# Sandwich attention layer: a slot's scores and first projected piece ahead of its output tiles, on TensorE and VectorE

## The chip, the cores and the metric

The kernel runs on one core of a Trainium2 chip. Times are microseconds of device time for one execution; the median of several runs counts. Engine names: PE is TensorE's matmuls and PEld its weight loads, DVE is VectorE, ACT is ScalarE, POOL is GpSimdE, SP is SyncE, which issues nearly all DMAs.

## What is computed

One transformer layer in sandwich form on x of 4 x 512 x 512: attention with 32 query heads and 8 key/value heads of 128 (weights are 4-bit codes times a scale per group of 128 rows), then a gated feed-forward part of width 1376 with 8-bit weights. Each part has a layer norm in front and behind and is added to its input.

```
q, k, v = [xn @ ((codes - 8) * repeat(scales, 128))  for q, k, v]     # xn = layernorm(x)
q, k = rope(q), rope(k);  k, v repeated 4 times over the heads
attn = softmax(q @ k.T * 128**-0.5 + causal_mask)
x = x + layernorm((attn @ v) @ dequant(o))
xn = layernorm(x)
x = x + layernorm((silu(xn @ gate.T * gs) * (xn @ up.T * us)) @ down.T * ds)
```

## The kernel before

Every factor is held as a high and a low float16 half, so a product is two or three matmuls. The attention part is 32 units of work, a unit U being one key/value head for one batch b = U % 4. A unit has four slots h = 0 to 3, one for each query head n = 4U + h, 128 slots in all. The order of each engine's work in a slot is written out by hand, engine by engine, and the engines meet at semaphores.

In slot n TensorE does, in this order: attend for head n-2 (L891, probabilities times V, 30 matmuls of 128 columns into ps_o), the scores of head n+1 in three groups (L876, into three banks ps_s), four output tiles of an earlier head through the output weights (L870, two matmuls of 512 columns each, named O0 to O3), and one or two pieces of the next unit's projection (L838, eleven matmuls of 512 columns for K and Q0 to Q3; L854, 48 of 128 columns for V). The pieces are dealt out by `FULL` (L76): slot 0 has K and Q0, slot 1 has Q1, slot 2 has Q2 and V, slot 3 has Q3. In the last unit `LAST` (L77) puts turned rows Y and X in their place. The scores' groups and the first three tiles alternate, then come the pieces, then O3.

Tiles and pieces share `ps_p`, a ring of four PSUM banks. `slot_sequence` (L82) gives the order of the entries in a slot; `bank_of` (L100) gives entry e of a unit the bank (22 x parity + e) % 4, and `bank_free` (L945) lets TensorE wait until the entry four places back has been read: for a tile VectorE's addition into y (o_add), for a piece VectorE's second reading or, for V, its low half (piece_dve). O0 also waits for ot_in: the head's output must have been normalized (ScalarE L703, L707), split (GpSimdE L554, o_low) and transposed by a DMA that SyncE issues (L428).

VectorE in a slot: `lows` (L1210, reads the score banks), the additions `add_output` (L1203, L1208) of the tiles, a reciprocal (L1227), and `take` (L1176) for each rope piece: it reads the bank once into `other` (L1191) and once into `rot` (L1195). The second reading also waits for GpSimdE to be done with the `rot` buffer (`rope_low`, L532, L538, writes k_lo or q_lo from it). There are three such buffers: K and Q2 share one, Q1 and Q3 another. A piece's two halves are swapped by DMA, added on GpSimdE one slot later (L530), made into the high half on ScalarE (L668), and into the low half on GpSimdE two slots later, behind that slot's p_lo (L546) and o_low. In slot 1 GpSimdE also dequantizes a weight block (L561, L564). At the end of slot 3 VectorE makes the low half of a weight block (`w_low`, L1104, L1108); in batch 3 the next K projection waits for it.

Of the kernel before, what the change touches and what calls it, by code (L numbers as in the profile page):

```python
# [80 lines left out]

def slot_sequence(pieces):  # L82

    return ("O0", "O1", "O2") + pieces + ("O3",)


def sequence(slots):
# [7 lines left out]
def place(slots, h, name):  # L95

    return sum(len(slot_sequence(p)) for p in slots[:h]) + slot_sequence(slots[h]).index(name)
# [71 lines left out]
def layer(nc, x, w_codes, w_scales, o_codes, o_scales,  # L169
# [3 lines left out]
    with ctx:  # L173
# [649 lines left out]
        def _(pe):  # L823
# [116 lines left out]
            def unit(U, b, slots, last=False, first=False):  # L940
                r = b % 2
                names = sequence(slots)
                idle = place(slots, 3, "O0") if first else 0

                def bank_free(e):  # L945


                    if first and e < RING + idle:
                        skipped = [x for x, name in enumerate(names[:idle]) if name[0] == "O"]
                        used = [x for x in range(e) if x not in skipped and bank_of(r, x) == bank_of(r, e)]  # L950
                        pe.wait_ge(piece_dve, len(START) + sum(q[0] in "KVQ" for q in names[:used[-1] + 1]) if used
                                   else len(START))
                        return
                    back = e - RING
                    ahead = names[back] if back >= 0 else sequence(FULL)[back]
                    if back < 0:
                        tail = sequence(FULL)[back + 1:] if back < -1 else ()
                        outs = outs_before(U) - sum(q[0] == "O" for q in tail)
                        pieces = pieces_before(U) - sum(q[0] in "KVQ" for q in tail)
                    else:  # L960
                        outs = outs_before(U) + sum(q[0] == "O" for q in names[:back + 1])
                        pieces = pieces_before(U) + sum(q[0] in "KVQ" for q in names[:back + 1])
                    if ahead[0] == "O":
                        after(pe, o_add, outs)
                    elif ahead[0] == "Y":
                        pe.wait_ge(y_read, int(ahead[1]) + 1)
                    elif ahead[0] == "X":
                        pe.wait_ge(m_xlo, int(ahead[1]) + 1)
                    else:
                        pe.wait_ge(piece_dve, pieces)  # L970

                def out_tile(n, h, nt):
                    if first and h < 3:
                        return
                    e = place(slots, h, f"O{nt}")
                    bank_free(e)
                    if nt == 0:
                        pe.wait_ge(ot_in, 16 * (n - 2))
                    if h < 3:
                        output(U - 1, h + 1, (h + 1) % 2, nt, bank_of(r, e))  # L980
                    else:
                        if first:
                            pe.wait_ge(o_cent, 1)
                        elif b == 0 and nt == 0:
                            pe.wait_ge(o_cent, U + HG)
                        output(U, 0, 0, nt, bank_of(r, e))

                for h in range(HG):
                    n = U * HG + h
                    more = not (last and h == HG - 1)  # L990
                    nxt = (n + 1, U, r, h + 1) if h < HG - 1 else (n + 1, U + 1, (r + 1) % 2, 0)
                    if h > 1:
                        attend(n - 2, r, h % 2, pieces_before(U - 1) + START.index("V") + 1)
                    elif not first:
                        attend(n - 2, 1 - r, h % 2, pieces_before(U - 2) + START.index("V") + 1)
                    if more:
                        scores(*nxt, 0)
                    out_tile(n, h, 0)
                    if more:
                        scores(*nxt, 1)  # L1000
                    out_tile(n, h, 1)
                    if more:
                        scores(*nxt, 2)
                    out_tile(n, h, 2)
                    for piece in slots[h]:
                        e = place(slots, h, piece)
                        if first and h == 0:
                            pe.wait_ge(xt_lo, NT)
                        bank_free(e)
                        bank = ps_p[:, bank_of(r, e), :]  # L1010
                        if piece[0] == "Y":
                            turn_y(int(piece[1]), bank)
                        elif piece[0] == "X":
                            turn_xn(int(piece[1]), bank)
                        else:
                            if b == NB - 1 and piece == START[0]:
                                pe.wait_ge(w_lod, U + 5)
                            if piece == "V":
                                project_v(U + 1, (b + 1) % NB, bank_of(r, e))
                            else:  # L1020
                                project(U + 1, (b + 1) % NB, piece, bank_of(r, e))
                    out_tile(n, h, 3)

            unit(0, 0, FULL, first=True)
            unit(1, 1, FULL)
# [77 lines left out]
        def _(dve):  # L1103
# [216 lines left out]
            def unit(U, b, slots, last=False, first=False):  # L1320
# [10 lines left out]
                for h in range(HG):  # L1331
                    n = U * HG + h
                    hp = (h + 1) % 2
                    more = not (last and h == HG - 1)
                    for g in range(NG):
                        if more:
                            lows(n + 1, hp, g)
                        out_tile(h, g)
                    invert(n, h)
                    if last and h:  # L1340
                        rows_add(h - 1)
                    for piece in slots[h]:
                        if piece[0] == "X":
                            xn_low(int(piece[1]), ps_p[:, bank_of(r, place(slots, h, piece)), :])
                    for V, vpar, piece, bank, taken in made(U, r, h, slots):
                        if piece != "V":
                            take(V, vpar, piece, bank, taken)
                    out_tile(h, 3)
                    for V, vpar, piece, bank, taken in made(U, r, h, slots):
                        if piece == "V":  # L1350
                            take(V, vpar, piece, bank, taken)
                    if h == 3 and not last:
                        w_low(U + 5, exact=(b + 5) % KT == EXACT)
                    if last and h:
                        to_xn(h - 1)
                    if last:
                        rows_first(h)
# [132 lines left out]
```

## Time and profile before

| | us |
|---|---|
| median of 3 runs | 1477.96 (1477.52 to 1479.47) |
| the profiled execution | 1479.83, its span 1478.0 |
| TensorE busy | 1386.7 (94%) |
| VectorE busy | 1115.5 (75%) |
| GpSimdE busy | 996.5 (67%) |
| ScalarE busy | 987.1 (67%) |

TensorE is at nine tenths or more of nearly every slice between the start-up and the end. A busy share tells which engine to look at; what a change of order is worth is read from the waits of that engine and from the rows of single slots. In the rows of a timeline the columns are start in us, duration in us, engine, line, operation, out<-in with the shape, count, and in brackets the idle time of that engine before it and what ended it.

### The profile page before, as it was taken

The page shows a single profiled execution, that of the slowest core. Times are in us where ns is not written, and L with a number is a line of the kernel's source. Part 1 is how long each engine was busy: PE and PEld are TensorE (multiplying, and loading weights), DVE is VectorE, ACT ScalarE, POOL GpSimd, SP SyncE. Part 2 cuts the span into 40 slices and gives each one's busy share as a digit, 9 for nine tenths or more (in the row PEclk, how much of TensorE's full clock was granted, in tenths as well). Part 3 has the DMA queues.
Part 4 walks back from the last instruction along what each step waited for, and adds up shares of the span by engine and source line. Part 5 has one row for each costly group of instructions (what it writes and reads, how often), then busy time and mean ns, then how long its engine had stood idle before and what let it go on. Part 6 is the DMA issues. An engine that isn't in the chain of part 4 may idle for free.

```text
span 1478.0 us, 33061 instructions
## 1 busy us (share of the span) xinstructions
PE 1386.7 (94%) x10944; PEld 837.3 (57%) x10944; DVE 1115.5 (75%) x2480; ACT 987.1 (67%) x2582; POOL 996.5 (67%) x710
## 2 busy tenths in 40 slices
PE   3689999999999999999999999999999968999998
PEld 1455665656656666666666665666666643454543
DVE  7856787777777878777777877788878795686744
ACT  2468777777777878877877887778777853241321
POOL 2369888888878888888888888888888751010100
PEclk9899999999999999999999999999999988999999
DMA  7389999999998998998899989899999854011000
GB/s 231 80 171 173 172 173 179 171 189 178 186 171 180 170 177 171 171 174 165 166 167 180 173 171 172 172 169 187 175 165 179 154 104 81 16 43 51 8 30 29
DMA packets 523323, 217.09 MB, mean 147 GB/s; under 512 B 479280, under 2 KB 481424, under 8 KB 523152
## 3 DMA queue, kind: packets, MB, share of 16 engines
q1 hardware_dynamic: 520592, 210.74, 72.9%
q0 software_dynamic: 2560, 4.23, 1.7%
q8 instruction: 88, 1.44, 0.4%
q14 instruction: 83, 0.68, 0.2%
HBM read 55.44 MB, written 4.29 MB: 40 GB/s over the span
## 4 chain that ended last, share of the span: by engine, by line
PE 63%; SPq 10%; DMA 9%; issue 6%; POOL 4%; DVE 4%; ACT 3%; POOLq 0%; DVEq 0%; ACTq 0%
DMA ot<-o_parts 7%; PE ps_p L848 6%; PE ps_p L849 6%; PE ps_p L873 5%; PE ps_p L874 5%; PE ps_p L851 5%; PE ps_s L1083 4%; PE ps_s L1082 4%; SPq L419 4%; PE ps_s L888 3%; PE ps_s L886 3%; PE ps_s L887 3%; PE ps_o L904 3%; PE ps_o L902 3%; PE ps_o L903 3%
## 5 line engine op out<-in xcount | busy, mean ns | idle before, releaser
L546 POOL TENSOR_TENSOR p_lo<-prob,p_hi 128x1280 f16<-128x1280 f32 x128 | 335.9, 2624 | 113.2 <-ACT p_hi L695 91.6
L1208 DVE SCALAR_TENSOR_TENSOR y<-ps_p,wo_scale,y 128x512 f32<-128x512 f32 x512 | 380.5, 744 | 32.8 <-PE ps_p L874 32.2
L686 ACT ACTIVATE prob<-prob,exp_bias 128x512 f32<-128x512 f32 (+3 forms) x512 | 285.5, 558 | 12.4
L1221 DVE CUSTOM_DVE_ANT_0 prob<-ps_s,mask 128x512 f32<-128x512 f32 (+3 forms) x512 | 236.7, 482 | 39.0 <-PE ps_s L888 38.6
L848 PE MATMUL ps_p<-x_hi,w_hi 128*128 128x512 f16 x640 | 244.5, 382 | 5.5 <-DVE w_lo L1108 3.9
L849 PE MATMUL ps_p<-x_lo,w_hi 128*128 128x512 f16 x640 | 244.4, 382 | 0.0
L873 PE MATMUL ps_p<-ot,wo 128*128 128x512 f16 x512 | 197.6, 386 | 36.7 <-DMA ot<-o_parts 27.6
L902 PE MATMUL ps_o<-v_hi,ffn_w 128*128 128x128 f16 x1280 | 221.8, 219 | 0.0
L903 PE MATMUL ps_o<-v_lo,ffn_w 128*128 128x128 f16 x1280 | 221.8, 219 | 0.0
L904 PE MATMUL ps_o<-v_hi,ffn_w 128*128 128x128 f16 x1280 | 221.7, 219 | 0.0
L530 POOL TENSOR_TENSOR rot<-rot,swap 128x512 f32<-128x512 f32 x160 | 202.6, 1275 | 24.8 <-DMA swap<-other 24.7
L1191 DVE SCALAR_TENSOR_TENSOR other<-ps_p,factor,sin 128x512 f32<-128x512 f32 x160 | 119.0, 744 | 107.0 <-PE ps_p L851 105.9
L874 PE MATMUL ps_p<-ot,wo 128*128 128x512 f16 x512 | 197.8, 386 | 0.0
L587 POOL TENSOR_TENSOR rstd<-ve,minus_half 128x1 f32<-128x1 f32 x48 | 26.4, 550 | 249.5 <-DVE ve L1280 249.5
L554 POOL TENSOR_TENSOR o_parts<-o_f,o_parts 128x512 f16<-128x512 f32 x128 | 161.4, 1261 | 44.5 <-ACT o_parts L707 43.9
L695 ACT ACTIVATE p_hi<-prob 128x1280 f16<-128x1280 f32 x128 | 162.7, 1271 | 33.3 <-DMA ffn_w<-p_hi 19.0
L851 PE MATMUL ps_p<-x_hi,w_lo 128*128 128x512 f16 x480 | 183.2, 382 | 0.0
L703 ACT ACTIVATE o_f<-ps_o,inv_sum 128x128 f32<-128x128 f32 x512 | 144.8, 365 | 44.6 <-PE ps_o L904 44.4
L886 PE MATMUL ps_s<-k_hi,q_hi 128*128 128x512 f16 (+3 forms) x512 | 153.9, 301 | 13.3 <-POOL q_lo L538 10.9
L887 PE MATMUL ps_s<-k_lo,q_hi 128*128 128x512 f16 (+3 forms) x512 | 153.8, 300 | 0.0
L538 POOL TENSOR_TENSOR q_lo<-rot,q_hi 128x512 f16<-128x512 f32 x128 | 149.6, 1169 | 1.7 <-ACT q_hi L668 1.7
L888 PE MATMUL ps_s<-k_hi,q_lo 128*128 128x512 f16 (+3 forms) x512 | 147.1, 300 | 0.0
(113 smaller groups left out, 2945.7 us busy)
## 6 DMA issues: line engine op xcount, KB each, us to landing
swap<-other SPq DMA_DIRECT2D x320, 128.0 KB, 2.8
w_code<-w_codes SPq DMA_DIRECT2D x36, 384.0 KB, 3.5
w_scale<-scratch SPq DMA_DIRECT2D x36, 384.0 KB, 5.2
o_code<-o_codes SPq DMA_DIRECT2D x35, 256.0 KB, 3.1
swap<-x SPq DMA_DIRECT2D x16, 256.0 KB, 2.8
out<-z SPq DMA_DIRECT2D x16, 256.0 KB, 2.0
ffn_w<-x SPq DMA_DIRECT2D x3, 1024.0 KB, 9.5
ffn_w<-p_hi SPq DMA_TRANSPOSE x128, 3.7
```

The costliest lines, as they stand in the source:

```text
L546: pool.tensor_tensor(p_lo[:, :], prob[:, hp, :], p_hi[:, :], ALU.subtract).then_inc(p_lod, 1)
L686: act.activation(prob[:, hp, a:a + w], prob[:, hp, a:a + w], ACT.Exp, bias=exp_bias[:, hp, i:i + 1], scale=-1.0, accum_out=exp_sum[:, hp, ...
L848: pe.matmul(ps_p[:, bank, :], wh, xh, start=(k == 0), stop=False)
L849: mm = pe.matmul(ps_p[:, bank, :], wh, xl, start=False, stop=False)
L851: mm = pe.matmul(ps_p[:, bank, :], wl, xh, start=False, stop=(k == KT - 1))
L873: pe.matmul(ps_p[:, bank, :], w, flat(ot[:, hp, 0:TT, :]), start=True, stop=False)
L874: pe.matmul(ps_p[:, bank, :], w, flat(ot[:, hp, TT:2 * TT, :]), start=False, stop=True).then_inc(o_ps, 1)
L902: pe.matmul(o, ph, vh, start=(i == ORDER[0] and j == 0), stop=False)
L903: pe.matmul(o, ph, vl, start=False, stop=False)
L904: mm = pe.matmul(o, pl, vh, start=False, stop=(i == ORDER[-1]))
L1208: dve.scalar_tensor_tensor(tile, ps_p[:, bank, :], scale, tile, ALU.mult, ALU.add).then_inc(o_add, 1)
L1221: dve.tensor_tensor_reduce(prob[:, hp, P_AT[i]:P_AT[i] + w], ps_s[:, bank, col:col + w], mask[:, S - w:], -SCORE_SCALE, NO_MINIMUM, ALU.ad ...
```

## The change

The entries of a slot get a new order: the first piece, then O0, O1, O2, then the second piece if there is one, then O3. TensorE does all three groups of scores before the first entry. VectorE does all score readings, then the reciprocal, then follows the new order of entries; V is taken last, as before. `slot_sequence` is also what the ring's banks and `bank_free` are worked out from, so the banks move with it.

```diff
 def slot_sequence(pieces):
 
-    return ("O0", "O1", "O2") + pieces + ("O3",)
+    return pieces[:1] + ("O0", "O1", "O2") + pieces[1:] + ("O3",)
...
                     if more:
-                        scores(*nxt, 0)
-                    out_tile(n, h, 0)
-                    if more:
-                        scores(*nxt, 1)
-                    out_tile(n, h, 1)
-                    if more:
-                        scores(*nxt, 2)
-                    out_tile(n, h, 2)
-                    for piece in slots[h]:
-                        e = place(slots, h, piece)
+                        for g in range(NG):
+                            scores(*nxt, g)
+                    for entry in slot_sequence(slots[h]):
+                        if entry[0] == "O":
+                            out_tile(n, h, int(entry[1]))
+                            continue
+                        e = place(slots, h, entry)
...
-                    out_tile(n, h, 3)
...
-                    for g in range(NG):
-                        if more:
+                    if more:
+                        for g in range(NG):
                             lows(n + 1, hp, g)
-                        out_tile(h, g)
                     invert(n, h)
                     if last and h:
                         rows_add(h - 1)
-                    for piece in slots[h]:
-                        if piece[0] == "X":
-                            xn_low(int(piece[1]), ps_p[:, bank_of(r, place(slots, h, piece)), :])
-                    for V, vpar, piece, bank, taken in made(U, r, h, slots):
-                        if piece != "V":
-                            take(V, vpar, piece, bank, taken)
-                    out_tile(h, 3)
-                    for V, vpar, piece, bank, taken in made(U, r, h, slots):
-                        if piece == "V":
-                            take(V, vpar, piece, bank, taken)
+                    taken_now = {item[2]: item for item in made(U, r, h, slots)}
+                    for entry in slot_sequence(slots[h]):
+                        if entry[0] == "O":
+                            out_tile(h, int(entry[1]))
+                        elif entry[0] == "X":
+                            xn_low(int(entry[1]), ps_p[:, bank_of(r, place(slots, h, entry)), :])
+                        elif entry in taken_now and entry != "V":
+                            take(*taken_now[entry])
+                    if "V" in taken_now:
+                        take(*taken_now["V"])
```

In the rows of the order below, the word in brackets is the semaphore that an instruction waits for: piece_dve tells that VectorE has read a piece, o_add that it has added a tile, ot_in that a head's transpose has landed, rot_lo that GpSimdE is done with a rope buffer.

TensorE in slot 2 of a middle unit, around the end of Q2 (L848 to L851) and the start of V (L865); before:

```order
L848 MATMUL ps_p<-x_hi,w_hi 128x512
L849 MATMUL ps_p<-x_lo,w_hi 128x512
L851 MATMUL ps_p<-x_hi,w_lo 128x512
L865 MATMUL ps_p<-w_hi,x_hi 128x128 [waits o_add]
L866 MATMUL ps_p<-w_lo,x_hi 128x128
```

and with the change:

```order
L851 MATMUL ps_p<-x_hi,w_lo 128x512
L873 MATMUL ps_p<-ot,wo 128x512 [waits ot_in,o_add]
L874 MATMUL ps_p<-ot,wo 128x512
L873 MATMUL ps_p<-ot,wo 128x512 [waits o_add]
L874 MATMUL ps_p<-ot,wo 128x512
L873 MATMUL ps_p<-ot,wo 128x512 [waits o_add]
L874 MATMUL ps_p<-ot,wo 128x512
L865 MATMUL ps_p<-w_hi,x_hi 128x128 [waits piece_dve]
```

Three tiles now stand between Q2 and V, and V waits for a piece instead of a tile.

TensorE in slot 1 of a middle unit, around the end of Q1 and the last tile O3; before (L902 is the next slot's attend):

```order
L849 MATMUL ps_p<-x_lo,w_hi 128x512
L851 MATMUL ps_p<-x_hi,w_lo 128x512
L873 MATMUL ps_p<-ot,wo 128x512 [waits o_add]
L874 MATMUL ps_p<-ot,wo 128x512
L902 MATMUL ps_o<-v_hi,ffn_w 128x128 [waits pt_lo_in,piece_dve,pt_hi_in,oq_norm]
```

and with the change:

```order
L851 MATMUL ps_p<-x_hi,w_lo 128x512
L873 MATMUL ps_p<-ot,wo 128x512 [waits ot_in,o_add]
L874 MATMUL ps_p<-ot,wo 128x512
L873 MATMUL ps_p<-ot,wo 128x512 [waits piece_dve]
L874 MATMUL ps_p<-ot,wo 128x512
L873 MATMUL ps_p<-ot,wo 128x512 [waits o_add]
L874 MATMUL ps_p<-ot,wo 128x512
L873 MATMUL ps_p<-ot,wo 128x512 [waits piece_dve]
L874 MATMUL ps_p<-ot,wo 128x512
```

All four tiles stand behind Q1, and the fourth, O3, waits for a piece.

VectorE in slot 2 of a middle unit, from the last score readings on; before:

```order
L1221 ISA low 128x1
L1208 SCALAR_TENSOR_TENSOR y<-ps_p,wo_scale,y 128x512 [waits o_ps]
L1227 RECIPROCAL inv_sum<-exp_sum 128x4 [waits exp_done]
L1191 SCALAR_TENSOR_TENSOR other<-ps_p,factor,sin 128x512 [waits piece_ps,swap_in0]
L1195 SCALAR_TENSOR_TENSOR rot<-ps_p,factor,cos 128x512 [waits rot_lo]
L1208 SCALAR_TENSOR_TENSOR y<-ps_p,wo_scale,y 128x512 [waits o_ps]
L1181 SCALAR_TENSOR_TENSOR v_lo<-ps_p,v_hi 128x512 [waits v_hid]
```

and with the change (its lines are four lower from here on):

```order
L1217 ISA low 128x1
L1223 RECIPROCAL inv_sum<-exp_sum 128x4 [waits exp_done]
L1187 SCALAR_TENSOR_TENSOR other<-ps_p,factor,sin 128x512 [waits piece_ps,swap_in0]
L1191 SCALAR_TENSOR_TENSOR rot<-ps_p,factor,cos 128x512 [waits rot_lo]
L1204 SCALAR_TENSOR_TENSOR y<-ps_p,wo_scale,y 128x512 [waits o_ps] x4
L1177 SCALAR_TENSOR_TENSOR v_lo<-ps_p,v_hi 128x512 [waits v_hid]
```

The two readings of Q2 stand ahead of all four additions of the slot.

## Rows read from the trace of the kernel before

**Rows 1.** Stretches: length, busy time (instructions) by engine, granted clock, DMA share, GB/s.

```profile
95.99:99.40 3.41, 3.35 (x11) 1.55 (x12) 2.24 (x5) 2.93 (x8) 2.38 (x1) 0.50 0.95 234
...
102.70:1171.90 1069.20, 1046.17 (x9092) 659.89 (x9090) 837.33 (x1920) 845.58 (x2295) 898.96 (x609) 1.00 0.92 174
```

**Rows 2.** Timeline of TensorE: first attend matmul of four slots.

```profile
102.76 0.22 PE L902 MATMUL ps_o<-v_hi,ffn_w 128*128 128x128 f16 x1
...
801.19 0.22 PE L902 MATMUL ps_o<-v_hi,ffn_w 128*128 128x128 f16 x1
...
835.87 0.22 PE L902 MATMUL ps_o<-v_hi,ffn_w 128*128 128x128 f16 x1
...
1171.94 0.22 PE L902 MATMUL ps_o<-v_hi,ffn_w 128*128 128x128 f16 x1
```

**Rows 3.** TensorE's waits, 102.7 to 1171.9: total us, times, longest.

```profile
PE ps_p L873 <- DMA ot<-o_parts: 17.1, 21, 1.8
...
PE ps_p L848 <- DVE w_lo L1108: 1.0, 2, 0.7
```

**Rows 4.** Timeline of TensorE in one short slot.

```profile
828.47 0.22 PE L902 MATMUL ps_o<-v_hi,ffn_w 128*128 128x128 f16 x1
...
830.14 0.38 PE L886 MATMUL ps_s<-k_hi,q_hi 128*128 128x512 f16 x1
...
833.07 0.38 PE L848 MATMUL ps_p<-x_hi,w_hi 128*128 128x512 f16 x1
...
835.22 0.38 PE L851 MATMUL ps_p<-x_hi,w_lo 128*128 128x512 f16 x1
835.44 0.38 PE L873 MATMUL ps_p<-ot,wo 128*128 128x512 f16 x1
```

**Rows 5.** VectorE: timeline of two pieces' readings; its waits for pieces, 102.7 to 1171.9.

```profile
801.19 0.75 DVE L1191 SCALAR_TENSOR_TENSOR other<-ps_p,factor,sin 128x512 f32<-128x512 f32 x1 [0.93 <-PE ps_p L851]
801.86 0.74 DVE L1195 SCALAR_TENSOR_TENSOR rot<-ps_p,factor,cos 128x512 f32<-128x512 f32 x1
...
835.86 0.75 DVE L1191 SCALAR_TENSOR_TENSOR other<-ps_p,factor,sin 128x512 f32<-128x512 f32 x1 [0.93 <-PE ps_p L851]
...
DVE other L1191 <- PE ps_p L851: 98.9, 112, 1.6
```

**Rows 6.** Timeline: TensorE waiting for VectorE's w_low, batch 3.

```profile
1032.50 2.94 DVE L1108 SCALAR_TENSOR_TENSOR w_lo<-w_scale,w_hi 128x768 f16<-128x768 f32 x1
...
1035.59 0.38 PE L848 MATMUL ps_p<-x_hi,w_hi 128*128 128x512 f16 x1 [0.30 <-DVE w_lo L1108]
```

**Rows 7.** Timeline of GpSimdE from slot 1 to k_lo in slot 2; VectorE's wait.

```profile
797.70 1.16 POOL L554 TENSOR_TENSOR o_parts<-o_f,o_parts 128x512 f16<-128x512 f32 x1 [1.13 <-ACT o_parts L707]
...
805.32 2.62 POOL L546 TENSOR_TENSOR p_lo<-prob,p_hi 128x1280 f16<-128x1280 f32 x1
...
809.02 1.16 POOL L538 TENSOR_TENSOR k_lo<-rot,k_hi 128x512 f16<-128x512 f32 x1
...
810.32 0.75 DVE L1195 SCALAR_TENSOR_TENSOR rot<-ps_p,factor,cos 128x512 f32<-128x512 f32 x1 [0.62 <-POOL k_lo L538]
...
DVE rot L1195 <- POOL k_lo L538: 20.8, 25, 1.1
```

**Rows 8.** VectorE: all w_low (ns min/median/max), score readings to reciprocal, reciprocal to reading.

```profile
L1108 DVE SCALAR_TENSOR_TENSOR w_lo<-w_scale,w_hi x32: 279/2596/3381, 66.7 to 1173.9; 128x768 f16<-128x768 f32 x24, 128x128 f16<-128x128 f32 x8
...
84.34 0.69 DVE L1221 CUSTOM_DVE_ANT_0 prob<-ps_s,mask 128x512 f32<-128x512 f32 x1 [0.17 <-PE ps_s L888]
...
85.99 0.17 DVE L1227 RECIPROCAL inv_sum<-exp_sum 128x4 f32<-128x4 f32 x1
...
827.42 0.16 DVE L1227 RECIPROCAL inv_sum<-exp_sum 128x4 f32<-128x4 f32 x1
827.50 0.72 DVE L1191 SCALAR_TENSOR_TENSOR other<-ps_p,factor,sin 128x512 f32<-128x512 f32 x1
```

**Rows 9.** Timeline of TensorE: two waits and what it did next.

```profile
94.63 0.39 PE L886 MATMUL ps_s<-k_hi,q_hi 128*128 128x512 f16 x1 [2.77 <-POOL q_lo L538]
...
234.40 0.38 PE L873 MATMUL ps_p<-ot,wo 128*128 128x512 f16 x1 [1.53 <-DMA ot<-o_parts]
```

More of the change, by code:

```diff
@@ L1010, in unit @@
                         bank = ps_p[:, bank_of(r, e), :]
[L1011 to L1014, printed above, removed]
+                        if entry[0] == "Y":
+                            turn_y(int(entry[1]), bank)
+                        elif entry[0] == "X":
+                            turn_xn(int(entry[1]), bank)
                         else:
-                            if b == NB - 1 and piece == START[0]:
+                            if b == NB - 1 and entry == START[0]:
                                 pe.wait_ge(w_lod, U + 5)
-                            if piece == "V":
+                            if entry == "V":
                                 project_v(U + 1, (b + 1) % NB, bank_of(r, e))
                             else:
-                                project(U + 1, (b + 1) % NB, piece, bank_of(r, e))
-                    out_tile(n, h, 3)
+                                project(U + 1, (b + 1) % NB, entry, bank_of(r, e))
             unit(0, 0, FULL, first=True)
@@ L1341, in unit @@
                         rows_add(h - 1)
-                    for piece in slots[h]:
-                        if piece[0] == "X":
-                            xn_low(int(piece[1]), ps_p[:, bank_of(r, place(slots, h, piece)), :])
-                    for V, vpar, piece, bank, taken in made(U, r, h, slots):
-                        if piece != "V":
-                            take(V, vpar, piece, bank, taken)
-                    out_tile(h, 3)
-                    for V, vpar, piece, bank, taken in made(U, r, h, slots):
-                        if piece == "V":
-                            take(V, vpar, piece, bank, taken)
+                    taken_now = {item[2]: item for item in made(U, r, h, slots)}
+                    for entry in slot_sequence(slots[h]):
+                        if entry[0] == "O":
+                            out_tile(h, int(entry[1]))
+                        elif entry[0] == "X":
+                            xn_low(int(entry[1]), ps_p[:, bank_of(r, place(slots, h, entry)), :])
[3 more added lines that the diff above has]
+                        take(*taken_now["V"])
                     if h == 3 and not last:
```

## Prediction

> **What bounds the kernel now.** I read the granted clock and busy time of the long middle stretch first, then TensorE's waits in it, then one slot row by row. From 102.70 to 1171.90 us TensorE is busy 1046 of 1069 us at a granted clock of 1.00, the 2.4 GHz level [rows 1]. The stretch is 30 units of four slots (units 1 to 30), from the first attend row at 102.76 to the one at 1171.94, 1069.2 us or 35.64 us a unit; a unit in which TensorE never waits lasts 835.87 - 801.19 = 34.68 us [rows 2]. So everything this stretch can give back is 1069.2 - 30 x 34.68 = **28.8 us**. Most of it is the wait of the first output tile for the transposed heads (17.1 us, 21 times); the weights' low halves cost 1.0 us [rows 3]. TensorE is the bound, and a change of its order is worth what it does to TensorE's waits.
>
> A slot in TensorE's rows [rows 4]: attend 828.47 to 830.14, 1.67 us; scores and three tiles up to 833.07, 2.93 us; a projection of eleven matmuls 833.07 to 835.44, 2.37 us; the last tile 0.43 us (835.44 to 835.87 [rows 2]). Three tiles are 1.29 us, so the scores are 2.93 - 1.29 = 1.64 us. This short slot is 7.40 us.
>
> **What the change does.** No instruction is added or removed; TensorE's and VectorE's order changes, ScalarE's, GpSimdE's and SyncE's does not. The first piece now starts 1.67 + 1.64 = 3.31 us into a slot instead of 4.60, the first tile at 5.68 instead of 2.32.
>
> *The wait for the transposed heads.* O0 starts 3.36 us later in its slot; the longest such wait in the stretch is 1.8 us [rows 3]. It goes, and I take all 28.8 us as given back (bounds 20 and 28.8: the 17.1 and a few others, or all).
>
> *The ring.* ps_p has four banks and an entry waits until the one four places ahead of it is read. Before, the pieces stood behind the tiles, and the entry after a lone piece took a tile's bank. Now the sequence is piece, O0, O1, O2, next entry, so the entry after O2 (Q0, O3, V, O3 in slots 0 to 3) takes the first piece's bank, and nothing but three tiles covers its reading. VectorE reads a rope piece twice, and the second reading frees the bank. Counted from the start of the piece's last matmul: VectorE starts 0.64 us later even when idle (835.22 [rows 4] to 835.86), as it was 112 times in the stretch; the second reading starts 0.67 after the first (801.19 to 801.86) and takes 0.74 [rows 5]; TensorE follows 0.15 us after VectorE's end (1032.50 + 2.94 = 1035.44 to 1035.59) [rows 6]. Sum 2.20 us. TensorE has 0.22 of that matmul left (835.22 to 835.44) and 1.29 of tiles, 1.51 us. **The floor of the new wait is 0.69 us in every slot**, because nothing is left on TensorE to hide it and the entry heads its queue: the rest of the slot and the next attend stand behind.
>
> The Trainium skill, "Perfetto Trace Analysis", section Optimizing Tensor Performance, Matmuls, says that independent groups should rotate through PSUM banks so that one's evacuation overlaps the next one's matmuls. The ring still rotates here; by that rule alone the sum would be the 1449 us of the third rival. By the rows the rotation comes round 0.69 us too soon.
>
> Slots 1 and 3: 0.69 each, 2 x 30 x 0.69 = **41.4 us**.
>
> Slot 2 (Q2, then V) costs more. The second reading of Q2 waits for GpSimdE to finish k_lo, which used the same rope buffer. Before, that ends at 809.02 + 1.16 = 810.18, 8.99 us into the slot, and VectorE goes on at 810.32, 0.14 later; VectorE waited for it 25 times in 30 units [rows 7]. There it hid behind V and O3 on TensorE; now V itself waits. GpSimdE's run up to k_lo is unbroken from slot 1's o_low at 797.70 [rows 7], which starts on that slot's attend; slot 1 becomes 0.69 longer, so k_lo ends 8.99 - 0.69 = 8.30 into slot 2. Then 0.14 + 0.75 + 0.15 = 1.04 to V's start at 9.34. TensorE is ready at 3.31 + 2.37 + 1.29 = 6.97. The wait is 2.37 us, 30 x 2.37 = **71.1 us**. Bounds: 0.69 a slot if k_lo comes in time, 2.37 + 0.69 = 3.06 if GpSimdE does not gain on the slot; the rows of the unbroken run decide for 2.37.
>
> Slot 0 (K, then Q0) has w_low ahead of it on VectorE, at the end of slot 3. There the second reading ends at 5.46 + 0.64 + 0.67 + 0.74 = 7.51; four additions at the same spacing of 0.67 bring w_low to about 10.1, which is 2.0 into slot 0, slot 3 being 7.40 + 0.69 = 8.09 long. w_low takes 0.28 to 3.38 us, median 2.60; it is the short form in one unit of four [rows 8]. The score readings up to the reciprocal take 85.99 - 84.34 = 1.65 us when no addition stands between them, and a piece's reading starts 0.08 after the reciprocal (827.42 to 827.50) [rows 8]. With 2.60 the reading of K starts at 2.0 + 2.6 + 1.73 = 6.33, against 5.46 + 0.64 = 6.10 from TensorE: 0.23 more than the floor, so 0.9 us in 16 units, and 0.69 in the 7 with the short form. In the other 7 (batch 3) K's matmuls wait for w_low itself; K's place was 4.60 and is 3.31, so they wait until 2.0 + 2.6 + 0.15 = 4.75, 1.44 us, and Q0 then 0.69. Sum 16 x 0.9 + 7 x 0.69 + 7 x 2.13 = **34.1 us** (bounds 30 x 0.69 = 20.7, and with 3.38 every time 16 x 1.7 + 7 x 0.69 + 7 x 2.91 = 52.4).
>
> Units 0 and 31, eight slots outside the stretch, I charge the floor: 8 x 0.69 = **5.5 us** (bounds 0, where other waits hide it, and 20, since in unit 31 the first entry is a Y that ScalarE reads only behind its exponentials).
>
> Sum: 41.4 + 71.1 + 34.1 + 5.5 - 28.8 = **+123.3 us**. The profiled execution took 1479.83 us and becomes 1603.1; it lies 1.87 above the median of the runs, 1477.96, so the forecast is **1601 us**.
>
> **Rivals.**
> 1. *GpSimdE gets ahead.* With 39 us a unit instead of 35.6, GpSimdE might reach k_lo before Q2 is read. Then slot 2 pays the floor: 30 x (2.37 - 0.69) = 50 us less, 1551. For it: the longer slots. Against: o_low is released by the attend of its own slot, so the run starts again in each slot 1.
> 2. *The clock falls.* TensorE stood 2.77 us before 94.63, and the stretch from 95.99 to 99.40 was granted 0.50, the 1.2 GHz level; a stand of 1.53 us before 234.40 changed nothing, since the stretch of rows 1 is at 1.00 [rows 1, 9]. My 2.37 lies between. Such a low stretch, 95.99 to 99.40, loses half of its length, 1.7 us; one in every slot 2 is 30 x 1.7 = 51 us more, 1652. For: the size of the wait. Against: TensorE is dense on both sides of it. [...]
> 3. *The tiles cover the reading (not slower).* If the two readings and their hops ended within 1.51 us of the last matmul's start, no entry would wait, and only the gain is left: 1477.96 - 28.8 = 1449. For: four banks still rotate, and VectorE is idle when the piece ends. Against: 2.20 from rows that repeat. It decides at 28.8 / 120 = 0.24 us a slot: below that the change gains.
>
> **How the numbers follow.** Forecast 1601, 74%, with its own range 1585 to 1635 from the bounds of slot 0, the ends and the gain. Rival 1 (1551) 11%, rival 2 (1652) 10%, rival 3 (1449) 2%, rival 3 in part, so that gain and wait cancel, 1%; 2% for a slower case beyond both. The range 1550 to 1640 holds the forecast and rival 1. 0.2% is about what a measurement of this kernel can tell from no change: faster 0.02, within 0.2% 0.01, slower 0.97.
>
> **What would show it.** Right: TensorE's waits on VectorE's second rope reading some 120 times, about 0.7 us before O3 in slots 1 and 3, about 2.4 before V; no wait of output tiles for the transposed heads; short slots of 8.1 us and a unit of 39 to 40 us; VectorE waiting for k_lo in slot 2. Wrong: a unit under 37 us, no waits on the readings, or a granted clock below 0.95 in the middle.

## The result, and the profile after

The changed kernel takes **1635.94 us** (median of 4 runs, 1634.89 to 1636.57) against 1478.72 for the kernel before beside it (1477.52 to 1479.71): ratio **1.1066**, interval 1.1049 to 1.1084. Slower, inside the range of 1550 to 1640 by 4 us, 35 us above the forecast of 1601. The profiled execution took 1634.89 us, 1633.1 of it span.

The page of the changed kernel: span, TensorE's busy time, and the granted clock in tenths over 40 slices.

```profile
span 1633.1 us, 33061 instructions
...
PE 1440.8 (88%) x10944; PEld 866.2 (53%) x10944; DVE 1100.1 (67%) x2480; ACT 988.5 (61%) x2582; POOL 984.9 (60%) x710
...
PEclk8889999999999999999999999999999987999999
```

The clock line looks harmless: a nine is all it shows for a slice at 0.9 or more. The stretches tell more. Columns as in [rows 1]; the first line is the middle, 30 units between two first attend rows, the second a piece of one slot 2.

```profile
108.10:1320.40 1212.30, 1095.83 (x9091) 683.32 (x9090) 821.55 (x1921) 847.38 (x2295) 886.82 (x608) 0.97 0.78 153
...
908.74:912.15 3.41, 3.41 (x30) 2.88 (x28) 0.58 (x1) 1.22 (x2) 2.62 (x2) 0.50 0.27 62
```

The middle was 1069.2 us at a clock of 1.00 [rows 1, 2]; it is 1212.3 at 0.97, so 143.1 of the span's 155.1 us were lost there. It begins 5.4 later (108.14 against 102.76) and 6.6 more are lost behind it. TensorE's busy time in it rose from 1046 to 1096 us with the same work, a sign that the clock fell: 0.50, the 1.2 GHz level, in the second line.

TensorE's waits in the middle (total us, times, longest), and VectorE's wait for k_lo. L865 is V's first matmul, L848 a rope piece's, L873 an output tile's; `rot` at L1191 is VectorE's second reading of a rope piece, `w_lo` its weights' low half.

```profile
PE ps_p L865 <- DVE rot L1191: 65.8, 30, 2.6
PE ps_p L873 <- DVE rot L1191: 22.3, 50, 0.9
PE ps_p L848 <- DVE rot L1191: 18.5, 30, 5.9
PE ps_p L848 <- DVE w_lo L1104: 5.6, 7, 0.8
PE ps_p L873 <- DMA ffn_w<-p_lo: 4.4, 10, 0.4
...
DVE rot L1191 <- POOL k_lo L538: 50.0, 30, 2.1
```

The wait for the transposed heads, 17.1 us over 21 times [rows 3], is gone. In its place TensorE waits in every slot for the second reading of the slot's own first piece: thirty times before V, thirty before Q0 (L848), and before O3 in the fifty and the ten (the 4.4 us in ten waits of 0.4 lie before O3 too and are as long as the others; the trace puts them down to a DMA). VectorE waits for k_lo in every slot 2, 50.0 us where it was 20.8 [rows 7].

One ring wait row by row: TensorE, then VectorE, in a slot 3 that begins at 912.17 (columns: start, duration, engine and line, operation; in brackets the idle time before and what ended it).

```profile
917.63 0.38 PE L851 MATMUL ps_p<-x_hi,w_lo 128*128 128x512 f16 x1
...
919.75 0.39 PE L873 MATMUL ps_p<-ot,wo 128*128 128x512 f16 x1 [0.44 <-DVE rot L1191]
...
920.19 0.22 PE L902 MATMUL ps_o<-v_hi,ffn_w 128*128 128x128 f16 x1
...
918.28 0.75 DVE L1187 SCALAR_TENSOR_TENSOR other<-ps_p,factor,sin 128x512 f32<-128x512 f32 x1 [1.62 <-PE ps_p L851]
918.95 0.74 DVE L1191 SCALAR_TENSOR_TENSOR rot<-ps_p,factor,cos 128x512 f32<-128x512 f32 x1
```

From the last matmul of the piece at 917.63: VectorE begins 0.65 later, reads again 0.67 later, for 0.74, to 919.69; TensorE goes on at 919.75, 0.06 after that. Together 2.12 us, of which TensorE's own work covers 1.51, so the floor is 0.61 and the slot 8.02 long (7.40 in [rows 4]). All 30 slots 3 and 28 of the slots 1 are 8.0.

Two slots 2 of the middle in TensorE's rows: the first attend, V's first matmul, and the next slot's first attend.

```profile
538.28 0.22 PE L902 MATMUL ps_o<-v_hi,ffn_w 128*128 128x128 f16 x1
...
547.60 0.23 PE L865 MATMUL ps_p<-w_hi,x_hi 128*128 128x128 f16 x1 [2.18 <-DVE rot L1191]
...
550.72 0.22 PE L902 MATMUL ps_o<-v_hi,ffn_w 128*128 128x128 f16 x1
...
898.08 0.22 PE L902 MATMUL ps_o<-v_hi,ffn_w 128*128 128x128 f16 x1
...
907.40 0.23 PE L865 MATMUL ps_p<-w_hi,x_hi 128*128 128x128 f16 x1 [2.19 <-DVE rot L1191]
...
912.17 0.22 PE L902 MATMUL ps_o<-v_hi,ffn_w 128*128 128x128 f16 x1
```

V starts 9.32 into each of them, after the same wait: 2.35 us from start to start, counted as in the prediction, and 2.18 or 2.19 in the brackets, which count idle time alone. But one slot is 12.44 long and the other 14.09. In the second the clock is 0.50 from 908.74 on, as above. Eleven of the thirty slots 2 are like the first and nineteen like the second, 1.63 us longer (14.06 against 12.43): **19 x 1.63 = 31 us**.

What holds V in the second: VectorE and GpSimdE.

```profile
904.18 0.75 DVE L1187 SCALAR_TENSOR_TENSOR other<-ps_p,factor,sin 128x512 f32<-128x512 f32 x1 [1.60 <-PE ps_p L851]
906.60 0.75 DVE L1191 SCALAR_TENSOR_TENSOR rot<-ps_p,factor,cos 128x512 f32<-128x512 f32 x1 [1.66 <-POOL k_lo L538]
...
905.29 1.16 POOL L538 TENSOR_TENSOR k_lo<-rot,k_hi 128x512 f16<-128x512 f32 x1
```

k_lo ends at 906.45, 8.37 into the slot, VectorE reads from 906.60 to 907.35, and V starts at 907.40.

### The profile page after: what moved, and what is told of

Its sections match the earlier page's. It is cut to its first block, busy times and chain, and to the rows that moved or that the text cites. A ratio compares the mean times of both kernels' runs of the same rounds, so it can differ in the third digit from the quotient of the medians.

```text
span 1633.1 us, 33061 instructions
## 1 busy us (share of the span) xinstructions
PE 1440.8 (88%) x10944; PEld 866.2 (53%) x10944; DVE 1100.1 (67%) x2480; ACT 988.5 (61%) x2582; POOL 984.9 (60%) x710
## 4 chain that ended last, share of the span: by engine, by line
PE 49%; issue 15%; POOL 14%; DVE 9%; DMA 5%; ACT 4%; SPq 4%; POOLq 0%; DVEq 0%; ACTq 0%
POOL rot L530 4%; PE ps_p L848 4%; DVE rot L1191 4%; PE ps_p L849 4%; PE ps_s L1078 3%; PE ps_s L1079 3%; PE ps_p L851 3%; PE ps_o L904 3%; PE ps_o L903 3%; PE ps_o L902 3%; PE ps_p L865 3%; POOL o_parts L554 3%; PE ps_p L867 2%; PE ps_p L866 2%; POOL k_lo L538 2%
## 5 line engine op out<-in xcount | busy, mean ns | idle before, releaser
L1204 DVE SCALAR_TENSOR_TENSOR y<-ps_p,wo_scale,y 128x512 f32<-128x512 f32 x512 | 353.4, 742 | 82.6 <-PE ps_p L874 82.4
L686 ACT ACTIVATE prob<-prob,exp_bias 128x512 f32<-128x512 f32 (+3 forms) x512 | 285.4, 558 | 12.4
L554 POOL TENSOR_TENSOR o_parts<-o_f,o_parts 128x512 f16<-128x512 f32 x128 | 150.1, 1173 | 223.3 <-ACT o_parts L707 223.3
L848 PE MATMUL ps_p<-x_hi,w_hi 128*128 128x512 f16 x640 | 246.3, 385 | 29.7 <-DVE rot L1191 20.3
L1217 DVE CUSTOM_DVE_ANT_0 prob<-ps_s,mask 128x512 f32<-128x512 f32 (+3 forms) x512 | 220.9, 485 | 75.2 <-PE ps_s L888 74.1
L873 PE MATMUL ps_p<-ot,wo 128*128 128x512 f16 x512 | 198.1, 387 | 45.4 <-DVE rot L1191 22.7
L902 PE MATMUL ps_o<-v_hi,ffn_w 128*128 128x128 f16 x1280 | 225.8, 221 | 0.0
L903 PE MATMUL ps_o<-v_lo,ffn_w 128*128 128x128 f16 x1280 | 225.7, 221 | 0.0
L904 PE MATMUL ps_o<-v_hi,ffn_w 128*128 128x128 f16 x1280 | 225.6, 221 | 0.0
L851 PE MATMUL ps_p<-x_hi,w_lo 128*128 128x512 f16 x480 | 184.2, 384 | 0.0
L865 PE MATMUL ps_p<-w_hi,x_hi 128*128 128x128 f16 x512 | 119.0, 259 | 72.7 <-DVE rot L1191 72.7
L695 ACT ACTIVATE p_hi<-prob 128x1280 f16<-128x1280 f32 x128 | 162.6, 1271 | 33.0 <-DMA ffn_w<-p_hi 18.4
L1191 DVE SCALAR_TENSOR_TENSOR rot<-ps_p,factor,cos 128x512 f32<-128x512 f32 x160 | 119.0, 744 | 62.0 <-POOL k_lo L538 54.7
```

The lines of the kernel that those rows point to most:

```text
L554: pool.tensor_tensor(o_lo, o_f[:, :], o_hi, ALU.subtract).then_inc(oq_lod, 1)
L686: act.activation(prob[:, hp, a:a + w], prob[:, hp, a:a + w], ACT.Exp, bias=exp_bias[:, hp, i:i + 1], scale=-1.0, accum_out=exp_sum[:, hp, ...
L848: pe.matmul(ps_p[:, bank, :], wh, xh, start=(k == 0), stop=False)
L851: mm = pe.matmul(ps_p[:, bank, :], wl, xh, start=False, stop=(k == KT - 1))
L902: pe.matmul(o, ph, vh, start=(i == ORDER[0] and j == 0), stop=False)
L903: pe.matmul(o, ph, vl, start=False, stop=False)
```

## The experiments

Losses against the kernel before, from first attend rows of the traces (profiled executions, us), for all kernels that ran: ahead of the first of the 30 units, in them, behind them.

| kernel | ahead | middle | behind | median of the runs |
|---|---|---|---|---|
| the change | +5.4 | +143.1 | +6.6 | 1635.94 |
| change, wait before V filled | +4.6 | +111.8 | +6.5 | 1602.31 |
| change, k_lo first | +3.4 | +60.7 | +10.2 | 1553.21 |
| scores ahead, old ring order | -1.3 | -7.0 | +8.4 | 1479.04 |
| the same, on TensorE alone | -2.1 | -14.8 | +0.8 | 1467.70 |
| the same, on VectorE alone | -0.7 | +3.6 | +7.1 | 1489.27 |
| piece behind one tile | -3.3 | +8.9 | +5.0 | 1492.72 |
| piece behind one tile, k_lo first | +0.4 | +21.3 | +5.9 | 1506.10 |
| scores between the tiles, k_lo first | +3.9 | +186.5 | +18.4 | 1687.58 |

The kernel before took 1479.42 beside the second, third, fourth and seventh line, and 1478.92 beside the fifth, sixth and the last two. The profiled execution of the fifth line was its fastest, 1463.69.

**Is it the clock?** The theory: the wait itself costs 2.35 us a slot 2, and the clock's fall behind it another 31 us in all. The rival: these V's are slow for another reason than TensorE's stand. The changed kernel with eight matmuls put into V's wait, whose results nobody reads; V must come no earlier.

```diff
                         e = place(slots, h, entry)
+                        if entry == "V":
+                            pe.wait_ge(oq_norm, (n - 1) * TT)
+                            for _ in range(8):
+                                pe.matmul(ps_o[:, :], flat(by_half(w_hi)[:, bass.ds(((U + 1) >> 2) & 1, 1), KT - 1, QW + KW:GW]),
+                                          x_hi[:, KT - 1, ((b + 1) % NB) * S:((b + 1) % NB + 1) * S], start=True, stop=True)
```

> The changed kernel, with eight extra matmuls of 512 columns (8 x 0.216 = 1.72 us, result thrown away, into the bank of the attend's output) put in slot 2 between O2 and V, where TensorE waits 2.35 us for the reading of Q2. The wait itself stays. Theory, the granted clock: the changed kernel shows 20 stretches at 0.50 in its middle and 19 of 30 slots 2 at 14.06 instead of 12.43 us; with TensorE at work through most of the wait the clock stays at 1.00, all slots 2 last 12.43, and the kernel takes 1636 - 19 x 1.63 - 2 = 1603 us (1600 to 1608). Rival: the slow V comes from what TensorE reads or from VectorE and ScalarE around it, not from the wait ahead of it; then 1636 or more.

Measured 1602.31 us, ratio 1.0827 (1.0811 to 1.0844), 33.6 less than the change. Its middle, and its wait before V:

```profile
107.30:1288.40 1181.10, 1116.98 (x9333) 677.05 (x9331) 821.77 (x1921) 847.77 (x2295) 887.75 (x608) 1.00 0.81 157
...
PE ps_p L865 <- DVE rot L1196: 14.1, 30, 0.5
```

With TensorE kept busy, V comes no sooner (its slots 2 are 12.4 to 12.5 long, all thirty), but the clock of the middle is 1.00, and no slot 2 is one of the long ones. TensorE's longest stand before V is now 0.5 us. More work made the kernel faster: the clock is the cause of the 31 us.

**Is the wait in slot 2 that for k_lo?** The changed kernel, in which GpSimdE makes k_lo in slot 2 ahead of p_low and o_low; nothing else moves.

```diff
                     n = U * HG + h
+                    early = h == 2 and not last
+                    if early:
+                        rope_low(*made_two_before(U, r, h, slots)[0][:3])
                     p_low(n, h % 2)
...
-                        for V, vpar, piece, bank, taken in made_two_before(U, r, h, slots):
+                        for V, vpar, piece, bank, taken in made_two_before(U, r, h, slots)[early:]:
```

> The changed kernel, with one order changed on GpSimdE: in slot 2 k_lo goes ahead of p_low and o_low, so that the rope buffer of Q2 is free some 4.7 us into the slot instead of 8.37. Theory: slot 2's wait for the reading of Q2 falls from 2.35 to the floor of 0.61 that slots 1 and 3 show, VectorE no longer waits for k_lo, and with the long wait the low clock goes too: 1636 - 30 x 1.74 - 19 x 1.63 = 1553 us (1548 to 1562). Rival: the wait before V comes from VectorE's queue (the additions that stand behind the readings); then slot 2 keeps its length and the time stays above 1620. The 0.61 in the other slots stays by either.

Measured 1553.21, ratio 1.0478 (1.0448 to 1.0508). Its middle, and TensorE's waits in it (lines three higher than in the changed kernel):

```profile
106.10:1236.10 1130.00, 1067.47 (x9093) 655.28 (x9092) 821.80 (x1920) 844.68 (x2295) 889.03 (x608) 0.99 0.85 164
...
PE ps_p L876 <- DVE rot L1194: 24.4, 53, 1.0
PE ps_p L851 <- DVE rot L1194: 16.1, 30, 3.5
PE ps_p L868 <- DVE rot L1194: 13.0, 30, 0.4
```

All thirty slots 2 are 10.69 long, 0.60 above the wait-free 10.09. VectorE's wait for k_lo is no longer among its waits, and with the long stand the clock's falls in slots 2 are gone too. What stays is the floor, in every slot, with the longer slots 0 of batch 3: of the 157 us, k_lo is the cause of 83, the clock's 31 among them, and the ring's shorter wait of most of the rest.

**Is the loss the place of the piece or the new place of the scores?** The changed kernel with the old ring order, so that scores alone are ahead on both engines.

```diff
-    return pieces[:1] + ("O0", "O1", "O2") + pieces[1:] + ("O3",)
+    return ("O0", "O1", "O2") + pieces + ("O3",)
```

> One part of the change alone: all scores ahead of the tiles on TensorE and VectorE, but the entries in the order of before (O0, O1, O2, pieces, O3), so the ring is that of before. Theory: no entry waits for a piece's reading, O0 starts 3.31 instead of 2.32 us into a slot, and the wait for the transposed heads (17.1 us in the middle, at most 1.8 each) mostly goes: 1478.7 - 15 = 1464 us (1455 to 1470). Rival: putting the scores ahead is itself part of the loss, since VectorE gets its additions later and in a row; then 1479 or more.

Measured 1479.04 (10 runs), ratio 0.9991 (0.9980 to 1.0002): the same as before. So the piece ahead of the tiles costs the whole loss, 157 us. But the 15 us that I expected from the scores were missed. They are gained and lost again. TensorE's wait for the heads in the middle, then its row before Q0 in a slot 0, then VectorE ahead of it:

```profile
PE ps_p L873 <- DMA ot<-o_parts: 4.7, 9, 1.1
...
537.15 0.39 PE L848 MATMUL ps_p<-x_hi,w_hi 128*128 128x512 f16 x1 [0.51 <-DVE y L1204]
...
531.48 3.24 DVE L1104 SCALAR_TENSOR_TENSOR w_lo<-w_scale,w_hi 128x768 f16<-128x768 f32 x1
...
536.38 2.03 DVE L1204 SCALAR_TENSOR_TENSOR y<-ps_p,wo_scale,y 128x512 f32<-128x512 f32 x3
```

The wait for the heads fell from 17.1 to 4.7 us. But VectorE, late from w_low, now does all score readings before the first addition at 536.38, and Q0's bank is that of O0: TensorE waits for the addition, twelve times in the middle, 6.9 us. Behind the middle another 8.4 are lost.

**Which engine's order gains, and which loses?** The old ring order with scores ahead on one engine only: TensorE with VectorE's order left as before, and the reverse. The first is the kernel of the last run with this in VectorE's slot:

```diff
-                    if more:
-                        for g in range(NG):
+                    for g in range(NG):
+                        if more:
                             lows(n + 1, hp, g)
+                        out_tile(h, g)
...
```

> TensorE's part alone, without the piece: all scores ahead of the tiles on TensorE, VectorE's order and the entries' order as before. The run with the scores ahead on both engines lost its gain in slot 0, where VectorE, late from w_low, did all score readings ahead of the first addition and 13 slots came out 0.7 longer, and in unit 31 (5 us). Theory: with VectorE's old order O0's addition comes after one score reading again, slot 0 goes back to 9.78 in most units, the heads' wait stays mostly gone as in that run, and unit 31 is as before: 1479.4 - 17 = 1462 us (1456 to 1469). Rival: the wait for the heads only moves to another place of the same loop (SyncE's queue and the transposes), and 1475 to 1480 is what any order gives.

Measured **1467.70** (6 runs, 1463.69 to 1468.85), ratio **0.9919** (0.9894 to 0.9943): 0.8% faster than the kernel before, a small gain but clear of the noise. Its middle, and the two largest waits left in it:

```profile
100.60:1155.10 1054.50, 1043.34 (x9093) 662.43 (x9092) 845.24 (x1923) 843.33 (x2294) 902.51 (x610) 1.00 0.93 176
...
PE ps_p L873 <- DMA ot<-o_parts: 5.4, 9, 1.1
PE ps_p L848 <- DVE w_lo L1104: 2.4, 4, 0.6
```

O0 now starts 0.99 us later in its slot (3.31 for 2.32), which takes 12 of the 17 us from the wait for the heads, and with VectorE's first addition early again Q0's wait is gone.

The reverse is the kernel before with VectorE's block of the change:

```diff
-                    for g in range(NG):
-                        if more:
+                    if more:
+                        for g in range(NG):
                             lows(n + 1, hp, g)
-                        out_tile(h, g)
...
```

> VectorE's part alone, without the piece: all score readings ahead of the additions on VectorE, TensorE's order and the entries' order as before. Theory: TensorE's waits for the heads stay as before (17 us in the middle), and slot 0 gets 0.7 longer in some 13 to 20 units because an entry waits for O0's late addition, and unit 31 loses some 5: 1479.4 + 9 + 5 = 1493 us (1485 to 1498). Rival: VectorE's order is hidden by the four banks; 1478 to 1481.

Measured 1489.27, ratio 1.0071 (1.0047 to 1.0094). Its wait for the heads in the middle, and a wait behind the middle:

```profile
PE ps_p L873 <- DMA ot<-o_parts: 18.1, 24, 1.8
...
PE ps_p L918 <- DVE y L1208: 9.0, 3, 5.1
...
1209.00 2.83 DVE L1295 TENSOR_SCALAR y<-y,mv,rstd 128x512 f32<-128x512 f32 x1 [0.58 <-POOL rstd L587]
...
1214.43 2.06 DVE L1208 SCALAR_TENSOR_TENSOR y<-ps_p,wo_scale,y 128x512 f32<-128x512 f32 x3
...
1215.24 1.12 PE L918 MATMUL ps_p<-ident,rot 128*128 128x128 f32 x4 [5.08 <-DVE y L1208]
```

The heads' wait stays as it was, and behind the middle TensorE waits 9.0 us for additions at L918 (0.2 in the kernel before). The rows show the longest of these waits, in the last slot of unit 31, which has no score readings left: there the new order puts the additions behind `rows_add`, VectorE's norm of finished rows, from 1209.00 to 1214.43; before, the first three stood ahead of it. The sum came out inside its 1485 to 1498, but not its parts: +3.6 in the middle where 9 was expected, +7.1 behind it for 5.

Against their own runs of before the two engines' halves are -11.2 and +10.4; both together were -0.4. In the total they add up within the noise, but not wait by wait: with both, Q0 waits 6.9 us for additions in the middle; with TensorE's half alone it does not, and with VectorE's alone 1.9 us.

**Does one tile ahead of the piece cover its reading?** The piece behind O0; the bank it leaves is wanted only by O3 or by a second piece later.

```diff
-    return pieces[:1] + ("O0", "O1", "O2") + pieces[1:] + ("O3",)
+    return ("O0",) + pieces[:1] + ("O1", "O2") + pieces[1:] + ("O3",)
```

> The changed kernel with O0 moved ahead of the first piece: O0, piece, O1, O2, second piece if any, O3. The bank of the first piece then comes round behind O1, O2 and one more entry, not behind three tiles: in slots 0 and 2 the second piece covers its reading, in slots 1 and 3 O3 and the next slot's attend and scores. Theory, the ring: no wait for a piece's reading is left, k_lo's wait is hidden behind V again, the clock stays at 1.00, and O0 starts 3.31 us into the slot: 1455 to 1470 us, about the same as with the scores alone; batch 3's K at 3.74 waits some 0.5 us more for the weights' low half than at 4.60. Rival: it is the late tiles and the pieces ahead of them that cost, wherever the banks stand; then most of the loss stays, above 1560.

Measured 1492.72, ratio 1.0084 (1.0069 to 1.0099). The ring did as expected: slots 1 and 3 are 7.41 long, without a wait. But 1455 to 1470 was missed. TensorE's wait for w_low in the middle; then VectorE in a slot 2 that begins at 519.87, and O3 on TensorE:

```profile
PE ps_p L848 <- DVE w_lo L1104: 8.1, 7, 1.3
...
529.36 0.75 DVE L1191 SCALAR_TENSOR_TENSOR rot<-ps_p,factor,cos 128x512 f32<-128x512 f32 x1 [2.21 <-POOL k_lo L538]
...
530.17 0.39 PE L873 MATMUL ps_p<-ot,wo 128*128 128x512 f16 x1 [0.48 <-DVE rot L1191]
```

Here V covers most of the reading of Q2, but k_lo comes so late that O3 behind V still costs most slots 2 another 0.3 to 0.7 us, with VectorE's additions behind it in the queue. K, wanted 0.86 us earlier than before, waits 8.1 us for w_low in place of 1.0 [rows 3]. With VectorE's score readings in front, and a first slot of the middle of 16.7 us, the gain is used up.

**And with k_lo early as well?** The two edits together.

> One tile ahead of the piece (O0, piece, O1, O2, ...), the run that took 1492.7, with k_lo first on GpSimdE in slot 2. There slot 2 ran 10.39 instead of 10.09 in most units, as O3 waited for the reading of Q2 that k_lo held up. Theory: these 0.30 go, 30 x 0.3 = 9 us: 1483.5 us (1480 to 1488). Rival: the 0.3 comes from the additions' queue; unchanged at 1492.

Measured 1506.10, ratio 1.018 (1.0148 to 1.0212): a miss, slower than without k_lo first. TensorE's waits in its middle (lines three higher):

```profile
PE ps_p L851 <- DVE y L1207: 14.4, 17, 2.6
PE ps_p L851 <- DVE w_lo L1107: 12.1, 7, 3.8
PE ps_p L876 <- DMA ot<-o_parts: 7.6, 11, 1.5
```

Slots 2 became wait-free as expected (28 of 30 at 10.09). But on GpSimdE o_low now stands behind k_lo and p_low, so the heads are late again (7.6 us in eleven waits, eight of them in slot 3), and slots 0 pay 19 us more in waits for w_low and for additions; behind two of these, of 3.76 and 2.57 us, the clock fell as well. Why w_low comes later there I did not settle.

**Scores between the tiles, to cover the reading.** The piece first, but groups 1 and 2 of the scores behind O0 and O1 on both engines, with k_lo first.

```diff
                     if more:
-                        for g in range(NG):
-                            scores(*nxt, g)
+                        scores(*nxt, 0)
                     for entry in slot_sequence(slots[h]):
                         if entry[0] == "O":
                             out_tile(n, h, int(entry[1]))
+                            if more and entry in ("O0", "O1"):
+                                scores(*nxt, int(entry[1]) + 1)
                             continue
...
```

> The piece stays ahead of the tiles and in the same ring order as in the changed kernel, but the second and third group of scores stand between the tiles again (scores 0, piece, O0, scores 1, O1, scores 2, O2, next entry) and their readings on VectorE likewise; k_lo is first on GpSimdE in slot 2. The bank comes round at the same distance, three tiles, with 0.98 us of scores more to cover the reading. Theory, cover: need 2.11 (2.20 less the smaller hop) against 1.51 + 0.98, so slots 1 and 3 are back at 7.40 from 8.01. K now starts 2.32 into slot 0, so in batch 3 it waits up to 2.4 for the weights' low half (17 us in all), and the later score readings may cost elsewhere: about 1490 us (1470 to 1515). Rival: a bank that comes round after three tiles costs its 0.6 whatever stands between; then slots 1 and 3 keep 8.0 and the time is above 1515.

Measured 1687.58, ratio 1.1404 (1.1370 to 1.1438): far off the 1490 expected. VectorE, then GpSimdE, then TensorE in a slot 0 that begins at 571.24:

```profile
580.87 0.75 DVE L1195 SCALAR_TENSOR_TENSOR rot<-ps_p,factor,cos 128x512 f32<-128x512 f32 x1 [2.15 <-POOL q_lo L538]
...
575.88 2.62 POOL L546 TENSOR_TENSOR p_lo<-prob,p_hi 128x1280 f16<-128x1280 f32 x1 [4.83 <-ACT p_hi L698]
...
579.58 1.15 POOL L538 TENSOR_TENSOR q_lo<-rot,q_hi 128x512 f16<-128x512 f32 x1
...
581.68 0.39 PE L851 MATMUL ps_p<-x_hi,w_hi 128*128 128x512 f16 x1 [1.70 <-DVE rot L1195]
```

and the waits in its middle of ScalarE for score readings and of GpSimdE for p_hi:

```profile
ACT exp_bias L684 <- DVE low L1221: 347.5, 178, 4.2
POOL p_lo L546 <- ACT p_hi L698: 290.9, 66, 7.9
```

Late score readings make the exponentials late (347.5 us of waits against 57.8 in the kernel before), these ScalarE's p_hi, and GpSimdE stands 4.83 us for it (290.9 us in all against 85.0); p_low, o_low and q_lo follow, q_lo holds the rope buffer, and the second reading of the piece waits for it. Groups 1 and 2 of the score readings stand behind that reading in turn, so the delay feeds itself from slot to slot. The stand of 1.70 us in the slot shown is a short one: in 21 of the 30 slots 0 it is 3.00 us, and a clock of 0.50 came with 12 of these 21. So this run is no test of the cover alone. It shows that slots other than 2 can pay the price of slot 2 as soon as GpSimdE's run starts later.

## Why the prediction was right, and where it was off

The direction and the mechanism held: TensorE waits in every slot for the second reading of the slot's own first piece, and longest in slot 2, for k_lo. The range held too, but that is in part luck. It was drawn for the forecast and rival 1; the result lies 1 us above the forecast's own 1585 to 1635, and had the clock fallen in all thirty slots 2, another 11 x 1.63 us would have put it at 1654, outside. The terms, as losses above a wait-free middle of 30 x 34.68 us, with what the slots of the changed kernel add up to:

| term | forecast | measured |
|---|---|---|
| slots 1 and 3, the ring | 41.4 | 37.3 |
| slot 2, V behind k_lo | 71.1 | 101.6 |
| slot 0 | 34.1 | 33.1 |
| ahead of and behind the middle | 5.5 | 12.0 |
| waits of before that go (by the count: what is left stands in the slots) | -28.8 | -28.8 |
| sum | 123.3 | 155.2 |

**The step that failed** is "TensorE is dense on both sides of it", with which I gave the second rival 10%. V started 9.32 into the slot (forecast 9.34) and k_lo ended at 8.37 (8.30), so the wait of 2.35 was sized rightly (k_lo 0.07 later, the step from VectorE to TensorE 0.05 for 0.15); but behind it the clock fell in 19 of 30 slots, at 1.63 us each (the rival's price was 1.7). The rival came true in two thirds, 31 us of the 35. The rows had left 1.53 without and 2.77 with a fall, both as idle time in brackets; in that measure the wait before V is 2.18, still between the two and above the longest of before in the middle, 1.8 [rows 3]. Nothing in them put the chance of a fall as low as a tenth. With the wait filled, the kernel takes 1602.31, the forecast's 1601.

The Trainium skill, "TensorE: Matmul & The Clock Gate", section HAM oscillation, has each pass of its loop begin cold after a DMA wait of about 3 to 5 us. Here the wait is shorter and 19 of 30 V's ran into a low clock behind it; of the 21 stands of 3.00 us in the run with the scores between the tiles, 12 came with one. So the trace agrees with it in part: not every pass goes cold.

**Rival 1 was a real branch.** With k_lo in time slot 2 pays the floor, as that rival said: 1553 measured with k_lo first, 1551 forecast. In the kernel as changed GpSimdE does not get ahead, for the reason given: in the slots shown its run up to k_lo begins with slot 1's o_low at 893.98, for which it had stood 2.99 us.

**The ring.** 0.61 a slot instead of 0.69. The term that was off is the step from VectorE's end to TensorE: 0.15 in [rows 6], where the reader was a w_low of 2.9 us; behind the reading of a piece it is 0.06. In slots 1 and 3 that is the 4 us between forecast and measured; in slot 2 the later k_lo cancelled it. The Trainium skill, "Perfetto Trace Analysis", section Optimizing Tensor Performance, Matmuls, would have groups rotate through the banks so that a reading overlaps the next matmuls; the trace has the rotation and the wait together.

**Slot 0 came out right for partly wrong reasons.** VectorE with w_low between two slots of the changed kernel:

```profile
922.24 2.06 DVE L1104 SCALAR_TENSOR_TENSOR w_lo<-w_scale,w_hi 128x768 f16<-128x768 f32 x1
...
926.29 0.75 DVE L1187 SCALAR_TENSOR_TENSOR other<-ps_p,factor,sin 128x512 f32<-128x512 f32 x1 [0.26 <-PE ps_p L851]
```

w_low took 2.06 here, where I charged 2.60, so VectorE was waiting for K again when K was done: 22 slots 0 pay the floor alone (10.39) and the 7 of batch 3 pay 1.57 (11.35) and not 2.13. What I had left out is the first slot of the middle, 18.55 long in place of 9.78:

```profile
121.17 0.61 PE L848 MATMUL ps_p<-x_hi,w_hi 128*128 128x512 f16 x1 [5.89 <-DVE rot L1191]
...
120.36 0.75 DVE L1191 SCALAR_TENSOR_TENSOR rot<-ps_p,factor,cos 128x512 f32<-128x512 f32 x1 [5.37 <-POOL q_lo L538]
```

GpSimdE is behind there from the start-up, and the new ring puts that on TensorE, with the clock at 0.50 from 120.26 on. Together 22 x 0.61 + 7 x 1.57 + 8.8 = 33.2.

**The gain.** The heads' waits went, as said. The tensor-alone run shows what they are worth by themselves: the later O0 brings back 14.8 of the 28.8 us of the middle's waits in its profiled execution, its fastest, and 11.2 us of the kernel in the median.

**The ends** cost 12.0, inside their bounds of 0 to 20.

**Still open:** why the same stand of 2.35 us is followed by a low clock in nineteen slots and not in eleven (nor does a longer one settle it: 3.00 us, 12 of 21), and whether a cover of 0.61 us more, without moving scores, would make this order pay; the run meant for that changed GpSimdE's timing as well.

## What to carry to other kernels

Moving a piece ahead in a ring of banks moves its reader's deadline too: count what the producer does between the piece and the next use of its bank, and hold it against the whole reading, hand-overs and the reader's own waits (here for a third engine) included. If a change is made on two engines alike, time each engine's half alone: here one half gained 11 us, the other lost 10. And where a new wait on TensorE lies between one that the trace shows to be harmless and one behind which the clock fell, put a large chance on the fall, and price it.

## What the runs showed of the hardware that I had not expected

- A stand of TensorE of 2.35 us (2.18 of it idle in the brackets), once in a slot of 12.4 us, was followed by a granted clock of 0.50 in 19 of 30 cases, at 1.63 us each. Stands of 0.61 us, four in every unit, were followed by none: with k_lo first there is no fall in the middle after its first slot.
- A longer stand did not make the fall certain: in the run with the scores between the tiles, 12 of 21 stands of 3.00 us came with a clock of 0.50.
- Matmuls that nobody needs, put into such a stand, made the kernel 33.6 us faster.
- From VectorE's end to TensorE's next matmul it took 0.06 us behind a reading of a piece (919.69 to 919.75), against 0.15 behind w_low in [rows 6].
